# Attention with relative positions and routed experts on one core: relative-score units in tile order, one transposed-probability buffer, and values stored with gaps

## The reference

```python
q, k, v = heads(x @ Wq + bq), heads(x @ Wk + bk), heads(x @ Wv + bv)   # 16 heads of 16 features
scores = einsum('bhqd,bhkd->bhqk', q, k)
pos_emb = dist_emb[pos_l - pos_r + 255]                                 # a negative index counts from the end
rel_q = einsum('bhld,lrd->bhlr', q, pos_emb)
rel_k = einsum('bhrd,lrd->bhlr', k, pos_emb)
probs = softmax((scores + rel_q + rel_k) / 4)
ctx = einsum('bhqk,bhkd->bhqd', probs, v)
s = layernorm(ctx @ Wo + bo + x) * ln_gamma + ln_beta
...
x = x + n + (n @ mix_w + mix_b)                                         # experts: n = layernorm(x) * g1 + be1
combine = top 2 of softmax(layernorm(x) @ router_w)                     # 8 experts, hidden width 1024
h = silu(einsum('td,edf->tef', flat, w1) + b1)
out = einsum('te,ted->td', combine, einsum('tef,efd->ted', h, w2) + b2)
```

## Time and profile before

| What | Value |
|---|---|
| median of 3 runs | 2013.5 us (2002.44 to 2020.78) |
| the profiled execution, its own time | 2002.44 us |
| its span (first to last instruction) | 2000.9 us |
| project and route | 0 to 360 us |
| experts, blocks 0 to 4, no relative scores | 360 to 460 us |
| experts with relative scores | 460 to 1296 us |
| attention (first score product to the end) | 1313 to 2001 us |
| busy share of the span | PE 81%, PEld 59%, DVE 62%, ACT 56%, POOL 28% |
| mean granted clock of TensorE | 0.909 |

### The profile page before, as it was taken

One profiled execution on the slowest core, in us unless ns is written; L12 is line 12 of the kernel. 1 busy time (PEld: TensorE's weight loads), 2 busy tenths in 40 slices (PEclk: granted clock), 3 DMA queues, 4 the chain that ended last, 5 costly groups with the idle time before them and its releaser, 6 DMA issues. The chain is left out here.

```text
span 2000.9 us, 32700 instructions
## 1 busy us (share of the span) xinstructions
PE 1626.6 (81%) x11256; PEld 1180.2 (59%) x11256; DVE 1235.0 (62%) x3009; ACT 1129.1 (56%) x1994; POOL 560.9 (28%) x662
## 2 busy tenths in 40 slices
PE   5758620787999899989999899759999999999981
PEld 3325320676788778877887788635555555555540
DVE  6755561621565546454646465758988888888860
ACT  2433310125656374736564556259888888888960
POOL 1352446320000000101000000014253654555454
PEclk9887655898999899999999999969999999999995
DMA  6463445996887897999887877689989989999931
GB/s 208 169 210 108 137 134 178 234 277 201 302 295 251 276 331 258 327 333 377 298 307 247 278 247 269 243 275 316 330 266 324 295 281 333 293 288 329 313 115 42
DMA packets 227381, 514.96 MB, mean 257 GB/s; under 512 B 37328, under 2 KB 83920, under 8 KB 222736
## 3 DMA queue, kind: packets, MB, share of 16 engines
q1 hardware_dynamic: 201856, 410.03, 63.6%
q0 software_dynamic: 24208, 98.65, 14.8%
q10 hardware_dynamic: 1152, 4.19, 0.5%
HBM read 367.08 MB, written 199.23 MB: 283 GB/s over the span
## 5 line engine op out<-in xcount | busy, mean ns | idle before, releaser
L983 DVE TENSOR_TENSOR rel_out<-rl,rel_tile 128x1024 f32<-128x1024 f32 x256 | 400.4, 1569 | 358.2 <-PE rl L1036 326.8
L960 ACT COPY rel_tile<-rl 128x1024 f32<-128x1024 f32 x256 | 377.0, 1476 | 297.7 <-DVE rel_out L983 164.7
L1273 ACT ACTIVATE scores<-scores,row_least 128x512 f32<-128x512 f32 x512 | 366.0, 718 | 35.5 <-DVE row_least L1309 33.2
L1309 DVE CUSTOM_DVE_ANT_1 scores<-sc,rq 128x512 f32<-128x512 f32 x512 | 338.6, 686 | 68.5 <-issue 57.7
L1413 PE MATMUL pt<-ident,scores 128*128 128x128 f32 x2048 | 321.9, 281 | 32.8 <-ACT probsT L1280 25.3
L1057 PE MATMUL up<-rowsT,w_b 128*128 128x256 f32 x1280 | 317.5, 394 | 4.4 <-DVE rowsT L989 2.3
L1413 PEld LDWEIGHTS pt<-ident,scores 128*128 128x128 f32 x2048 | 249.0, 145 | 115.7 <-DVE probsT L1317 35.9
L1070 PE MATMUL dn<-w_b,hid 128*128 128x256 f32 x1280 | 307.8, 385 | 0.0
L1057 PEld LDWEIGHTS up<-rowsT,w_b 128*128 128x128 f32 x1280 | 237.9, 195 | 33.8 <-DVE rowsT L989 5.0
L1070 PEld LDWEIGHTS dn<-w_b,hid 128*128 128x128 f32 x1280 | 233.1, 191 | 25.9
L1405 PE MATMUL sc<-ks,qs 96*128 96x512 bf16 x512 | 204.2, 399 | 32.9 <-DMA ks<-scratch_parts 20.0
(11 more groups left out here) (188 smaller groups left out, 1670.5 us busy)
## 6 DMA issues: line engine op xcount, KB each, us to landing
scratch_rel<-rel_out SPq DMA_DIRECT2D x256, 512.0 KB, 3.8
rq<-scratch_rel SPq DMA_DIRECT2D x256, 512.0 KB
krows_sb<-scratch_stack SPq DMA_DIRECT2D x768, 64.0 KB, 3.1
w_b<-in_w POOLq DMA_DIRECT2D x40, 1152.0 KB
w_b<-in_w POOLq DMA_DIRECT2D x40, 1028.0 KB
scratch_parts<-part SPq DMA_DIRECT2D x96, 128.0 KB
qrows_sb<-scratch_stack SPq DMA_DIRECT2D x192, 64.0 KB, 3.3
qs<-scratch_parts SPq DMA_DIRECT2D x192, 64.0 KB
```

Of the source, the lines that this page charges most:

```text
L960: nc.scalar.copy(square(tile)[:, :, u * UN:(u + 1) * UN], rl[r][:].rearrange("p a (b l) -> p l (a b)", l=TILE)).then_inc(s_kc, 1)
L983: nc.vector.tensor_tensor(out[n % SRING][:], rl[r][:].rearrange("p a (b s) -> p (a b) s", s=TILE), square(tile)[:, u * UN:(u + 1) * UN], A ...
L1273: nc.scalar.activation(sm[j][:, i], sm[j][:, i], ACT.Exp, bias=least[:, j, i:i + 1], scale=-1.0, accum_out=es[:, g // 2 % 2, i, 2 * j + g ...
L1309: nc.vector.tensor_tensor_reduce(sm[j][:, i].rearrange("p (c s) -> p c s", c=LT), sc[i % 2][:].rearrange("p (c s) -> p c s", c=LT), rq[j][ ...
```

## The change

Three parts, in three stages.

1. Experts: the steps run in tile order. All 16 K units of a tile, then its 16 Q units, then the next tile. `step`, `STEP_OF` and `square` are gone, `rel_tile` is held one way round in every tile, and ACT's first K copy of a tile waits for all Q adds of the tile before. SP issues the eight `load_k` pieces ahead of the 16 stores of a tile.
2. Attention: one `probsT` buffer in place of two, held by head in even groups and by block in odd ones, so that block j of the context frees the places that head j of the next group writes. For this the context moves from behind the second transposition to the start of the head, ahead of its first scores. `scale_ctx` on DVE moves from i == 3 to i == 1.
3. Values: `va` has the gaps already. DVE clears both `va` buffers once in route, ACT writes each row tile in two copies of 128 columns instead of one of 256, and the stored tensor has twice the width. SP loads `vs` directly (512 KB per octet); POOL's `spread`, its two memsets and the `values` tile are gone.

The diff, cut to its core:

```diff
@@ route, take_v
-                    nc.scalar.copy(va[b % 2][:, i], vm[i][:, 0:E]).then_inc(s_va, 1)
+                        if b < 2:
+                            act.wait_ge(s_gap, b + 1)
+                    for half in range(2):
+                        dst = va[b % 2][:, i].rearrange("p (o q h c) -> p o q h c", o=2, q=2, c=2 * D)[:, :, half, :, half * D:(half + 1) * D]
+                        src = vm[i][:, 0:E].rearrange("p (o q h d) -> p o q h d", o=2, q=2, d=D)[:, :, half]
+                        ins = nc.scalar.copy(dst, src)
+                    ins.then_inc(s_va, 1)
@@ route, DVE
+            for i in range(2):
+                nc.vector.memset(va[i][:], 0.0).then_inc(s_gap, 1)
@@ experts, due
-                yield step(n)
+                tile, u = n // (2 * UNITS), n % (2 * UNITS)
+                yield u // UNITS, tile, u % UNITS, n % 2
@@ experts, SP
-            for p in range(PIECES - 1):
-                load_k(p + KRING)
             for tile in range(TILES):
+                for p in range(PIECES):
+                    x = tile * PIECES + p + KRING
+                    if x < TILES * PIECES:
+                        load_k(x)
                 for u in range(UNITS):
...
-                    x = ((tile + 1) * UNITS + u) // PER_PIECE - 1 + KRING
-                    if u % PER_PIECE == 0 and x < TILES * PIECES:
-                        load_k(x)
@@ experts, ACT
-                        if tile:
-                            act.wait_ge(s_qa, (tile - 1) * UNITS + u + 1)
-                        nc.scalar.copy(square(tile)[:, :, u * UN:(u + 1) * UN],
+                        after(act, s_qa, tile * UNITS)
+                        nc.scalar.copy(both[:, :, u * UN:(u + 1) * UN],
@@ experts, DVE
-                                                square(tile)[:, u * UN:(u + 1) * UN], ALU.add).then_inc(s_qa, 1)
+                                                both[:, u * UN:(u + 1) * UN], ALU.add).then_inc(s_qa, 1)
@@ attention
-        pT = [sb(f"probsT{i}", [P, HG, ST, S]) for i in range(2)]
+        pT = sb("probsT", [P, HG, ST, S])
-            return pT[g % 2][:, k, r]
+            return pT[:, k, r] if g % 2 == 0 else pT[:, r, k]
@@ attention, SP
-                        after(sp, s_vp, 2 * o)
+                        after(sp, s_pv, g // 2 - 1)
-                        sp.dma_start(vc[:], src[:, :, o % NO * cols:(o % NO + 1) * cols]).then_inc(s_vl, 16)
+                        sp.dma_start(vs[g // 2 % 2][:], src[:, :, g // 2 % NO * E:(g // 2 % NO + 1) * E]).then_inc(s_vs[g // 2 % 2], 16)
@@ attention, DVE
-                    if j == 3 and i == 3 and g and g % 2 == 0:
+                    if j == 3 and i == 1 and g and g % 2 == 0:
                         scale_ctx(g // 2 - 1)
@@ attention, PE
                 for i in range(ST):
+                    if i == 0 and g:
+                        context(g - 1, j)
                     if n + AHEAD < HEADS:
                         score(n + AHEAD, i)
                     turn(n, i)
-                    if i == 1 and g:
-                        context(g - 1, j)
```

62 lines of the change are left out of this document (17 added, 45 removed).

## The result

The changed kernel takes 2092.32 us (median of 4 runs, 2088.67 to 2105.03), the kernel before, timed beside it, 2011.66 (2002.44 to 2020.78): ratio 1.0406, 95% interval [1.0368, 1.0444]. It is slower by 81 us. Forecast were +22 us and, as the range, 1975 to 2092 us. The sign was right, the size was not, and the time lies just above the top of the range.

A forecast was written before the change was run, and what follows sets the result against it. PE was taken as nearly full in the experts, no engine as clearly the bound in attention. Experts -28, attention +48 and values +2 gave +22 us: 2024.4 on the profiled execution, 2035 predicted on the median, range 1975 to 2092.

The forecast's parts named there:

- attention: Attention stage: 45 us for DVE waits at 31 group starts, 18 after projections, 15 given back; +48 us, bounds 0 and +73.
- The floor: Experts with relative scores: at PE's floor half a tile takes 23.2 us, 31 halves 719, so at most 91 us won.
- Values: Route and the value loads: two narrower ACT copies cost 2 us, memsets and larger loads 0; sum +2 us.
- The experts: Experts with relative scores: 91 us won by tile order less 40, 15 and 8 given back; -28 us, bounds -91 and +50.
- Three things are given back: Experts: K row pieces 40 us, first pieces queued behind the last stores 15, DVE waits for stores 8.
- 13 us of slack: Experts, kernel before: K row pieces issued four K units ahead, units every 3.25 us; in the change 5.8 to 7.3 us.
- The median, 5.8, just fits: K row pieces: sixth issue some 2.7 us after the first, median landing 3.1 us, against slack of 5.8 to 7.3 us.
- With half the slack I take 40: K row pieces in the experts: long tiles before made up 23 us; with half the slack 40 us lost.
- 1 us in each of 15: Experts: the first pieces of a K half are queued behind the last stores, 15 us in all.
- Q half bound by its stores: Experts rival, slower by more: at 338 GB/s stores bind Q halves; experts +35, total +85, 2098 us; chance 0.15.
- the +50 bound: Experts' upper bound: at 338 GB/s each Q half takes 29.3 us instead of 23.2; 98 and weights 43 over 719.
- What would show it: Signs: copies near 1.0, adds 1.23, tiles 48 us, short K row waits; wrong if tiles take 46.5 or Q halves 29.

The follow-up runs named there:

- attention_only: The kernel before with part 2 alone (one `probsT` buffer, context at the head's start, `scale_ctx` earlier): 2057.47 us, ratio 1.0217.
- order_only: The kernel before with part 1 alone (tile order in the experts): 2058.1 us, ratio 1.0206 to the kernel before.

## Why the prediction was right and wrong

- **The direction, and attention: right.** The contexts were to cost +48 us; attention_only costs +44, the trace +39.5. The mechanism is the forecast's: DVE idle at a group's start, by 1.67 us in the row above instead of 1.45 and by 44 us in all over the 31 starts. In time it is worth some 34 us (1.1 each) instead of 45; where the rest is made up is not shown. The other places (a context behind the projection, less the gap given back) came out at +9, forecast +3.
- **Copies and adds: right.** 1.02 and 1.22 us throughout. **The floor: right,** and reached: 22.4 to 23.0 us in both halves of tiles 13 and 15 and in K halves 3 and 11, forecast 23.2. That all of the -91 us could be won is not shown: the shortest stage of any run is 778.3 us, with reload and half of the stores left out, and 779.6 with all the work, where 719 was the floor and before had 810.5.
- **Values: right.** +2 forecast, +3.5 measured, not to be told from none.
- **The experts: wrong,** -28 forecast, +32 in the trace (+48 in that of part 1 alone). The failed step is "Three things are given back", whose terms 40 + 15 + 8 = 63 us measured 123.5. Three faults in it:
  1. The reload of Q rows was in no term, though SP's line for it was in the code beside the moved `load_k`. It is 48 issues and 3.1 MB at each turn of a row. In the interleaved order the K pieces went out between its parts; in tile order they are behind all of it. The halves at the turns hold 63 of the 123.5 us; without the reload some 15 us of such a sum stay (66 in order_only). Leaving the reload out gave 59 us in part 1's order and 31 in before. I had put before's window of 57.8 us down to traffic; it was a turn of a row, and tiles 3 and 11 (58.3 and 53.3 us) were as well, which the period of four should have told. The "13 us of slack" of before did not hold there either: at tiles 4, 8 and 12 PE waited for pieces that were issued 8 to 12 us after their buffers were free.
  2. "The median, 5.8, just fits" took the median landing for a test of lead. The lead itself, 5.8 to 7.3 us, was right (5.3 to 7.3 in the trace). What counts is the tail, where weights and stores come by: issues and last landing then take 8.7 to 12.6 us, and the K halves that meet this lost 4 to 14 us. "With half the slack I take 40" had no working; one more buffer took 54 us off these K halves.
  3. "1 us in each of 15": what delays the awaited pieces is mostly the weights of the experts, which the forecast has only in its upper bound, and at the turns SP's list, by 13.3, 4.1 and 10.1 us.
- **The rival "Q half bound by its stores",** 2098 us, came nearest by number and not by mechanism. The 13 Q halves without a reload take 319.8 us together, 24.6 each and not 29.3; the two windows above have a DMA share of 0.93 and 0.99 at 356 and 373 GB/s. They are close to that bound, but do not pay much for it. Its +35 has no working in the forecast, and of its 1.5 MB of other traffic in a half the sum beside it gives 1.05; the +50 bound has the same term.
- **"What would show it"** named waits for K rows "shorter than 2 us each outside weight loads", a tile near 48 us, and as a sign of being wrong Q halves of 29 us. The first two failed: the twelve longest waits in after last 1.6 to 12.3 us, and a tile takes 54.4 us (842.7 over 15.5).

Settled by runs and their traces: what each part costs; what the reload costs; the lead; SP's list at the turns; the group's first context. Not explained: that the parts' sum is 12 us more than the whole (within their intervals). Supported by the number of packets in flight only: that a DMA with a repeated source uses few engines. Open: whether the new order can be faster than the old one at all, and the reload in a place that no list waits for.

## What to carry to other kernels

When an order is changed, list everything that the in-order queue behind it issues, not only the moved instruction: here the DMA that nobody moved (48 small issues per row of tiles) made up nearly half of what the experts' stage lost to its floor, since it now stood in front of the ones that are waited for. Bunching the same transfers into half of the time needs more lead; a ring that was deep enough for the spread order has to be judged by the longest landing, and one more buffer is the cheap test. Give the old order the same buffers, too, before crediting the new one: here the old order gained 26 us by them. Offloading issues to an engine that looks idle helps only as far as nothing in its own list is urgent.

## What the hardware showed that was not expected

- Loads of 256 KB into 16 partitions landed 1.9 us apart (138 GB/s) where stores of 512 KB from 128 partitions landed 1.2 us apart. Fewer and larger DMAs of that shape saved SP 24 us of issues per reload and cost 14 to 41 us in time.
- A DMA of 64 KB costs SP some 0.46 us of issue, while such DMAs land 0.3 to 0.5 us apart when they queue: 48 in a row (25.3 us) are slower to issue than the 22.5 us in which PE uses what they bring.
- A source repeated by a leading dimension of 3 or 2 left the DMA share at 0.38 while PE waited. The time rose by 23% over before, and in part 1's order by 21% over part 1 alone.
- What SP's queue was given landed nearly in its order, so that stores that land 1.2 us apart landed up to 25.9 us after their issue, behind the large loads.
